# A 16-head cross-attention on one Trainium2 core: loops unrolled, scores as three high/low products on two 64-row halves, one maximum over all heads, normalisation on ScalarE

## What is computed

```
query = _layernorm(x)
q = jnp.einsum('bsd,hdk->bhsk', query, Wq) + bq[None, :, None, :]
k = jnp.einsum('bsd,hdk->bhsk', key, Wk) + bk[None, :, None, :]
v = jnp.einsum('bsd,hdk->bhsk', value, Wv) + bv[None, :, None, :]
scores = jnp.einsum('bhqk,bhmk->bhqm', q, k) / jnp.sqrt(jnp.asarray(D_K, q.dtype))
scores = jnp.where(mask == 0.0, -1000000000.0, scores)
attn = jax.nn.softmax(scores, axis=-1)
h = jnp.einsum('bhqm,bhmk->bhqk', attn, v)
h = h.transpose(0, 2, 1, 3).reshape(query.shape[0], query.shape[1], N_UNITS)
x = x + (h @ Wo + bo)
```

## Time and profile before

| | |
|---|---|
| runs (3), median | 1867.78 us (1865.9 to 1868.61) |
| profiled execution, span from first to last instruction | 1867.0 us |
| instructions | 26853 |
| TensorE busy | 1470.1 us, 79% |
| TensorE weight loads | 1059.4 us, 57% |
| VectorE busy | 1136.3 us, 61% |
| ScalarE busy | 617.3 us, 33% |
| GpSimd busy | 267.5 us, 14% |
| mean granted TensorE clock | 0.853 of full |

### The profile page before, as it was taken

How to read it: one execution, slowest core, us unless ns; L and a number is a source line. 1 busy time by engine, 2 the same in 40 slices (tenths; PEclk the granted TensorE clock), 3 DMA queues, 4 the chain that set the end, 5 groups by cost and what they waited for, 6 DMA issues and landing times. The chain is left out here.

```text
span 1867.0 us, 26853 instructions
## 1 busy us (share of the span) xinstructions
PE 1470.1 (79%) x7749; PEld 1059.4 (57%) x7749; DVE 1136.3 (61%) x3732; ACT 617.3 (33%) x1055; POOL 267.5 (14%) x237
## 2 busy tenths in 40 slices
PE   3999977999967652206806998799999999879982
PEld 1666766989944442104504777466666666557771
DVE  5777664566648855731256886445555455478868
ACT  1444403444432210002204554233333333345541
POOL 1212100101001000271273220000000000022202
PEclk8999987999985555557857999799999999989995
DMA  6000000000000040004310000000000000000001
GB/s 211 1 0 0 1 0 1 1 1 0 1 1 1 0 150 0 3 38 127 99 37 5 1 0 1 1 1 1 1 1 0 0 1 1 1 1 0 0 1 46
DMA packets 38579, 34.21 MB, mean 18 GB/s; under 512 B 8672, under 2 KB 35552, under 8 KB 38112
## 3 DMA queue, kind: packets, MB, share of 16 engines
q1 hardware_dynamic: 35168, 26.78, 4.6%
q0 software_dynamic: 3328, 6.43, 1.0%
HBM read 24.14 MB, written 9.44 MB: 18 GB/s over the span
## 5 line engine op out<-in xcount | busy, mean ns | idle before, releaser
L484 POOL TENSOR_TENSOR mha_kbd<-KT,w_ctx 128x1024 f32<-128x1024 f32 x48 | 91.3, 1901 | 810.0 <-SPq L97 513.3
L1983 DVE SCALAR_TENSOR_TENSOR tree_hl<-tree_pH,tree_hh 128x512 fp32r<-128x512 f32 x192 | 132.3, 689 | 122.4 <-ACT tree_hh L1881 121.6
L392 PE MATMUL mha_pS<-mha_kbd,mha_qT 128*128 128x512 f32 x384 | 203.0, 612 | 4.3 <-ACT mha_qT L450 3.4
L425 PEld LDWEIGHTS mha_pO<-VB,mha_PT 128*128 128x128 f32 x1536 | 183.6, 193 | 10.8 <-issue 8.7
L425 PE MATMUL mha_pO<-VB,mha_PT 128*128 (+1 forms) x1536 | 178.7, 259 | 0.0
L1881 ACT ACTIVATE tree_hh<-tree_pH 128x512 fp32r<-128x512 f32 x192 | 114.6, 597 | 177.3 <-PE tree_pH L1784 177.3
L518 DVE TENSOR_REDUCE mha_nm<-mha_pS 128x8 f32<-128x512 f32 x192 | 131.5, 685 | 42.6 <-PE mha_pS L396 24.0
L521 DVE TENSOR_TENSOR mha_Z<-mha_pS,mha_nm 128x512 f32<-128x512 f32 x192 | 132.8, 692 | 19.3
L462 ACT ACTIVATE mha_PT<-mha_pT 128x1024 f32<-128x1024 f32 x96 | 98.3, 1024 | 136.8 <-PE mha_pT L407 136.6
L457 ACT ACTIVATE mha_PR<-mha_Z 128x1024 f32<-128x1024 f32 x96 | 101.5, 1057 | 85.4 <-DVE mha_Z L521 85.4
L407 PEld LDWEIGHTS mha_pT<-w_ctx,mha_PR 128*128 128x128 f32 x768 | 87.4, 141 | 38.4 <-issue 38.2
(11 more groups left out here) (421 smaller groups left out, 2828.9 us busy)
## 6 DMA issues: line engine op xcount, KB each, us to landing
w_tree_full<-in_tree_full_dram SPq DMA_DIRECT2D x1, 4224.0 KB, 13.9
exp_W<-in_L_W_dram SPq DMA_DIRECT2D x32, 128.0 KB, 2.3
slots_in<-route_zero SPq DMA_DIRECT2D x40, 64.0 KB, 1.9
w_rot<-in_rot_dram SPq DMA_DIRECT2D x1, 2307.0 KB, 8.7
X<-in_x_dram SPq DMA_DIRECT2D x8, 256.0 KB, 6.2
exp_xe<-slots_in SPq DMA_DIRECT2D x16, 128.0 KB, 2.9
slots_out<-exp_ye POOLq DMA_DIRECT2D x16, 128.0 KB, 2.8
out_dram<-X SPq DMA_DIRECT2D x8, 256.0 KB, 2.3
```

The source lines that it names most:

```text
L392: ins = pe.matmul(pS[:, n, :], qT[u][:, P * v:P * v + P], kbd[u][:, 8 * n:8 * n + 8, :], start=True, stop=not key_mask)
L425: ins = pe.matmul(pOv[:, c, :], PT[v][:, P * c:P * c + P], VB[:, a.b(-2), c, :], start=True, stop=True)
L484: pool.tensor_tensor(kbd[u][:], kb, bmask.unsqueeze(2).to_broadcast([P, H, SK]), ALU.mult).then_inc(s["kbd"], 1)
L1983: dve.scalar_tensor_tensor(hl[k % 2][:], pH[k % 2][:], 0.0, hh[k % 2][:], ALU.max, ALU.subtract).then_inc(s["lo"], 1)
```

## The change

- The slots are all written out (no loop, no registers).
- `q` and the keys are split into a high part, rounded to fp32r, and the remainder (`qh`, `ql`, `kh`, `kl`). The scores are the sum of three single-pass products, high x high, high x low, low x high. Rows 0 to 63 hold heads 0 to 7 and rows 64 to 127 heads 8 to 15, so every product is done as two of 64 rows and 512 columns, one for each half of `pS`. GpSimd makes `kf`, `kh`, `kl` of half of `kbd`'s width; ScalarE makes `qh`, VectorE `ql`.
- The key mask of layer 0 is two products of 64 rows, of which three in each half are not zero.
- VectorE takes the maximum of all 16 heads in one instruction and the shift in one. `scores(t)` waits for the whole shift of tile t-1, not for half of it.
- The normalisation goes to ScalarE (scale `RS`, bias `NB` = -mean x `RS`), `bn_aggr` writes `MV` directly and stands one slot later.
- The order within a slot changes on TensorE and VectorE.

The core of the diff (waits of the same form and the unrolled indices left out):

```diff
-        kbd = [st.sb(f"kbd{u}", [P, H, SK]) for u in range(2)]
+        kf = st.sb("kf", [P, HG, SK])
+        kh = [st.sb(f"kh{u}", [P, HG, SK], F32R) for u in range(2)]
+        kl = [st.sb(f"kl{u}", [P, HG, SK], F32R) for u in range(2)]
...
-                need(pe, s["Z"], 2 * t - 1 + n)
-                ins = pe.matmul(pS[:, n, :], qT[u][:, P * v:P * v + P],
-                                kbd[u][:, 8 * n:8 * n + 8, :], start=True, stop=not key_mask)
+                pe.wait_ge(s["q"], b + 1)
+                pe.wait_ge(s["kl"], b + 1)
+                need(pe, s["Z"], t)
+                q0 = slice(P * v, P * v + P)
+                for n, (qq, kk) in enumerate(((qh, kh), (qh, kl), (ql, kh))):
+                    for r in range(2):
+                        rows = slice(HR * r, HR * r + HR)
+                        ins = pe.matmul(pS[:, HG * r:HG * r + HG, :], qq[u][rows, q0], kk[u][rows, :, :],
+                                        start=(n == 0), stop=(n == 2 and not key_mask))
                 if key_mask:
-                    nb = core.nbias3[:, bass.ds(b, 1), :].to_broadcast([3, 8, SK])
-                    ins = pe.matmul(pS[:, n, :], core.ones3[:], nb, start=False, stop=True)
+                    for r in range(2):
+                        rows = slice(HR * r, HR * r + HR)
+                        nb = core.nbias[rows, b, :].unsqueeze(1).to_broadcast([HR, HG, SK])
+                        ins = pe.matmul(pS[:, HG * r:HG * r + HG, :], core.ones_b[rows, :], nb, start=False, stop=True)
...
+            def slot(t):
+                if live(t + 1):
+                    scores(t + 1)
+                if live(t - 1):
+                    turn(t - 1)
+                if live(t - 3):
+                    pe.wait_ge(s["at"], t - 2)
+                    need(pe, s["aT"], t - 3)
+                    pe.transpose(pA, at[(t - 3) % 2][:], ident).then_inc(s["aTp"], 1)
+                if t % 2 == 1 and live(t + 3):
+                    x_transposes((t + 3) // TB)
+                if t % 2 == 0 and live(t + 2):
+                    queries((t + 2) // TB)
+                if live(t - 2):
+                    attend(t - 2)
...
+            def normalise(b):
+                need(act, s["xTp"], b - 1)
+                for j in range(TB):
+                    t = TB * b + j
+                    ins = act.activation(xh[b % 2][:, j, :], X[:, t, :], ACT.Identity, bias=NB[:, t:t + 1], scale=RS[:, t:t + 1])
+                ins.then_inc(s["xh"], 1)
...
+                pool.tensor_tensor(kf[:], kb, bmask.unsqueeze(2).to_broadcast([P, HG, SK]), ALU.mult).then_inc(s["kf"], 1)
+                pool.wait_ge(s["kf"], b + 1)
+                pool.tensor_copy(kh[b % 2][:], kf[:]).then_inc(s["kh"], 1)
+                pool.wait_ge(s["kh"], b + 1)
+                pool.tensor_tensor(kl[b % 2][:], kf[:], kh[b % 2][:], ALU.subtract).then_inc(s["kl"], 1)
...
+                def q_low(b):
+                    dve.wait_ge(s["qh"], b + 1)
+                    need(dve, s["S"], 2 * b - 2)
+                    dve.scalar_tensor_tensor(ql[b % 2][:], pQ[:, 0:S], w("bq"), qh[b % 2][:], ALU.add, ALU.subtract).then_inc(s["q"], 1)
...
+                def slot(t):
+                    if live(t - 3):
+                        dve.wait_ge(s["O"], t - 2)
+                        dve.reciprocal(rc[t % 2][:], pOv[:, :, 2 * HD:VW]).then_inc(s["rc"], 1)
+                    if live(t + 1):
+                        largest(t + 1)
+                    if live(t - 3):
+                        need(dve, s["aTp"], t - 3)
+                        dve.wait_ge(s["rc"], t - 2)
+                        dve.tensor_tensor(at[(t - 3) % 2][:].rearrange("p (c h d) -> p c h d", h=2, d=HD),
...
+                    if live(t + 1):
+                        shift(t + 1)
```

More of the change, by code:

```diff
@@ L148, in token_scales @@
     return on_scalar, on_vector
[L151 to L192, removed]
 def prep_parts(core, L, key_mask, st, pk, pv):
@@ L388, in scores, with queries @@
-            def scores(t, b, u, v, n):
-                need(pe, s["q"], b + 1)
-                need(pe, s["kbd"], b + 1)
-                need(pe, s["Z"], 2 * t - 1 + n)
-                ins = pe.matmul(pS[:, n, :], qT[u][:, P * v:P * v + P],
-                                kbd[u][:, 8 * n:8 * n + 8, :], start=True, stop=not key_mask)
+            def queries(b):
+                pe.wait_ge(s["xT"], b + 1)
+                pe.matmul(pQ[:, 0:S], w("wq"), xT[b % 2][:], start=True, stop=True).then_inc(s["qp"], 1)
@@ L433, in _, with turn, attend @@
-            x_transposes(0, 0)
-            queries(0, 0)
-            scores(0, 0, 0, 0, 0)
-            scores(0, 0, 0, 0, 1)
-            x_transposes(1, 1)
-            tile_slots(pe, slot, 4)
+            def turn(t):
+                pe.wait_ge(s["P"], t + 1)
+                need(pe, s["PT"], t)
+                for c in range(CH):
+                    ins = pe.transpose(pT[:, P * c:P * c + P], PR[t % 2][:, P * c:P * c + P], ident)
+                ins.then_inc(s["PTp"], 1)
+            def attend(t):
+                pe.wait_ge(s["PT"], t + 1)
+                need(pe, s["at"], t)
+                for c in range(CH):
+                    ins = pe.matmul(pOv[:, c, :], PT[t % 2][:, P * c:P * c + P], VB[:, t // TB, c, :], start=True, stop=True)
+                ins.then_inc(s["O"], 1)
@@ L440, in _ @@
+            x_transposes(0)
+            queries(0)
+            for t in range(-1, T + 4):
+                slot(t)
         @blk.scalar
         def _(act):
-            def x_evac(b, u):
-                need(act, s["xTp"], b + 1)
-                need(act, s["qp"], b - 1)
-                act.activation(xT[u][:], pQ[:, 0:S], ACT.Copy).then_inc(s["xT"], 1)
-            def q_evac(b, u):
-                need(act, s["qp"], b + 1)
-                need(act, s["S"], 4 * b - 4)
-                act.activation(qT[u][:], pQ[:, 0:S], ACT.Identity, bias=w("bq")).then_inc(s["q"], 1)
@@ L479, in _ @@
+            rs_act(act)
+            act.wait_ge(s["nb"], 1)
+            normalise(0)
+            normalise(1)
+            x_evac(0)
+            q_evac(0)
+            for t in range(-1, T + 4):
+                slot(t)
         @blk.gpsimd
         def _(pool):
[L481 to L487 removed]
@@ L558, in _ @@
+                q_low(0)
+                for t in range(-1, T + 5):
+                    slot(t)
             rs_dve(dve)
+            dve.scalar_tensor_tensor(NB[:], MV[:, :, 0], -1.0, RS[:], ALU.mult, ALU.mult).then_inc(s["nb"], 1)
             if mask is None:
@@ L2285, in packs @@
         rest = np.float32(rest - neg3[i])
+    negs = np.zeros(P, np.float32)
+    for r in (0, P // 2):
+        negs[r:r + 3] = neg3
     out = {}
```

223 lines of the change are left out of this document (84 added, 139 removed).

## The result

The changed kernel takes 1881.02 us (median of 12 runs, 1867.61 to 1905.0) against 1869.28 us for the kernel before on the same chip (12 runs, 1865.15 to 1875.0). The ratio is 1.0064, with a 95% interval of 1.0039 to 1.0089. It is slower by some 0.6%, where 0.45% faster was forecast. The profiled execution of the change has a span of 1891.7 us at a mean granted clock of 0.818; that of before has 1867.0 and 0.853.

What follows compares the result with a forecast made beforehand. TensorE's queue alone was taken to bound attention before, a TensorE-VectorE loop after. Steady part -16.9, fill +9.3, first scores -0.2, tail -0.6 sum to -8.4 us: 1858.6 profiled, 1859.4 us median, 0.45% faster, range 1848 to 1883.

Steps and rivals of the forecast that it cites:

- The clock falls in the steady part, since TensorE now idles: Rival, attention's steady part: a slot at half clock costs some 4 us, one stage so over 50 us; chance 0.02.
- the lower clock reaching beyond the fifth tile: Sign that the forecast is wrong: TensorE's lower clock at a stage's start lasts past its fifth tile.
- the halves of a pair run side by side: Score products on TensorE: the two 64-row halves overlap, so the six span 0.57 us from first to last start.
- No overlap: Rival, score products: halves of a pair don't overlap, span 1.17 us, +0.60 a slot, 1917 us in all; chance 0.16.
- the weight-load rival: Score products: a half's weights aren't loaded while its own product streams, span 0.79 us, 1878 us in all; chance 0.08.
- the loop through the maximum and `at`: Attention slots: a loop through TensorE and VectorE sets the period, 5.07 us a tile, 5.30 in layer 0.
- The steady part: 28 slots of each attention stage: layer 0 -18.9 us, layers 2 and 3 +2.0 together, sum -16.9.
- the fill: First scores to those of tile 4: +3.7 us each in layers 2 and 3, +1.9 in layer 0, +9.3 in all.
- first scores: Stage starts: 0.6 us later for `q_low` and `NB`, less 0.4 in each of layers 2 and 3: -0.2 us.
- Tail: End of each attention stage: the copy of `MV` (0.2 us) goes, three times: -0.6 us.
- the unrolling at nothing: Attention loops written out: register instructions and longer straight code priced at nothing; code loading, if it shows, a few tenths a stage.
- VectorE doesn't bind: Attention slots: VectorE needs 3.8 us a tile and would need 1.3 more to bind; no chance of its own.

Runs made afterwards that it cites:

- the filler: Changed kernel plus three useless double-pass products a slot in TensorE's idle place, ahead of the wait for `at`: 1859.2 us, ratio 0.9956 to the kernel before.
- full rows: Changed kernel with VectorE's `at` ahead of the maximum, and scores and key bias in 128 rows instead of 64: 1861.52 us, ratio 0.9961 to the kernel before.
- Warm: Changed kernel with VectorE's `at` ahead of the maximum, plus useless TensorE products in waits of each stage's start and first slots: 1793.51 us, ratio 0.96 to before.
- before, unrolled: Kernel before with only the loops of its attention stages written out: 1868.57 us, ratio 1.0006 to the kernel before.
- at last: Changed kernel with VectorE's `at` of tile t-3 moved behind the shift of tile t+1 too: 2167.23 us, ratio 1.1601 to the kernel before.

## Why the prediction was wrong

**The step that failed** is the rival "*The clock falls in the steady part, since TensorE now idles* (0.02): a slot at half clock costs some 4 us; one stage so is over 50 us". The mechanism was named and put aside at 0.02. It was thought of as all or nothing: a whole stage at the lower clock, or none. What happens is small and frequent: mostly some 3 us at 1.2 GHz, in 20 of 84 slots of the profiled execution, 22.7 us in all, and then the tails of layers 2 and 3, 14.0 us with the little of layer 0. Together that is 36.7 us in the profiled execution and 22 us at the median (1881.0 against 1859.2 with the filler). The forecast gain was 8.4. The profile's own columns had the warning in them: the forecast put 0.7 us of idle time into each slot of an engine whose clock was 1.00 in the stretches where it was busy all the time, and 0.58 in the one at a stage's start; "the lower clock reaching beyond the fifth tile" stood among its signs of being wrong.

The Trainium skill ("TensorE: Matmul & The Clock Gate", A second HAM failure mode: psum-queue depth-cycling) tells of a kernel in which TensorE idles for a moment between groups of products, often enough that its clock goes down and up all the time. This case's trace agrees (0.50 us idle a slot, clock 0.90 to 0.93). That section was not weighed in the prediction; it speaks for the rival that was given 0.02.

Point by point:

- *Right: the halves of a pair run side by side.* The span of the six is 0.57 as taken, and "full rows" prices it. The two of a pair start together, though, and not 0.1 apart; the 0.1 lies between the first pair and the second (0.34, then 0.23). No overlap (a span of 1.17) and the weight-load rival (0.79) are out: the second pair's loads start 0.11 behind the first pair's products, in the same rows.

```profile
121.22 0.19 PEld L358 LDWEIGHTS mha_pS<-mha_kl,mha_qh 64*128 64x128 f32 x2
```

- *Right: the loop through the maximum and `at`.* 5.07 and 5.30 forecast, 5.1 and 5.3 measured in undisturbed slots. The idle time of 0.7 was reckoned from start to start; so read it is 0.66 (122.24 to 123.83, less 0.93 for the transposes), of which 0.50 are left when the last transpose has landed. The steady part was summed to -16.9. With the filler it is 430.3 against 447.2 of before: -16.9. The terms agree one by one, so this is no luck.
- *Right in kind, too large: the fill.* From the first scores to those of tile 4: 19.0, 19.3, 17.8 against 18.5 and 15.3 and 15.6 in layer 3, +6.7 instead of +9.3. "Warm" shows its cause: the lower clock in the first slots is worth 2 to 4 us a stage. The 18.5 of layer 0 hangs on when the clock rose in that one execution ("before, unrolled": 24.9), so the difference in layer 0 prices nothing by itself.
- *Wrong sign: first scores.* -0.2 forecast in all, +4.6 measured (+2.0, +1.0, +1.6). 1.1 us of it a stage is VectorE's product stretched beside GpSimd's new operations, which were priced for GpSimd alone; the rest I put down to the longer path (`NB`, `ql`), which no run here takes apart.
- *Tail.* -0.6 forecast; -1.5 measured from the last `rc` on, but +14.0 in the three slots ahead of it, all of it clock (8.8 each with the filler).
- *Right: the unrolling at nothing* ("before, unrolled", 1.0006, by the medians), and VectorE doesn't bind (101.00 of 156.00 us busy).

## What to carry to other kernels

When an engine with a clock that follows its activity is full, a change that shortens its work but puts a wait of half a microsecond into each round may not be worth what the loop says. Price the idle time as a cost of its own, and look for it in the granted clock by stretches, tails included, before the busy shares. Two cheap tests tell the wait from the clock: put useless work into the idle place (the waits stay, the clock comes back), and take the wait away by moving one instruction on the engine that is waited for. The saving of TensorE time by the row halves was real all along (59 us by "full rows"); it came out only when VectorE did `at` ahead of the maximum.

## What the chip did that I had not expected

- TensorE's clock dips for some 3 us at a time with only 0.50 us idle in a slot of 5.1 to 5.4. With 0.27 us the dips stay in layer 0 and the time falls by 10 us, with none to speak of they are gone. With an idle time of some 1.8 us a slot at full clock ("at last"; an estimate, 0.50 + 1.33) it is down for most of the time (0.57 to 0.61).
- A 32-element VectorE product of two SBUF operands, 0.19 us by itself, takes 1.14 to 1.27 us when it runs beside GpSimd's `kl` subtraction, and ends with it. The Trainium skill ("GPSIMD Engine Reference", Specifications) lists a shared way to SBUF for VectorE instructions with two SBUF inputs, and the trace agrees. The cast alone does it too: 1.06 us beside the cast of "full rows" (1.04 us).
- Products in rows 0 to 63 and 64 to 127 pair up in both orders tried: standing next to each other in the program, or three apart, they start within 0.01 us of each other.
